# Statistics of two sequences moved from the end of one stage into the next, and a bias split moved behind a plan

## The chip, the cores and the metric

The kernel runs on one core of a Trainium2 chip as one program. Its engines run side by side, each with its own list of instructions, and wait for one another on semaphores: PE (TensorE: matmuls and transposes), DVE (VectorE: elementwise work and reductions), ACT (ScalarE: activation functions), POOL (GpSimd: here products, small arithmetic and DMAs with computed addresses) and SP, which here only issues DMAs. The metric is device time of one execution in microseconds (us); lower is better.

## The reference, cut to what matters

Two transformer layers work on 16 sequences of 512 tokens with 128 features (as 64 tiles of 128 tokens, four to a sequence). Each layer modulates a layer norm, mixes over time, adds, modulates a second layer norm, and applies a mixture of experts:

```python
h = _layernorm(x) * (1 + ca) + sa          # layer 0
x = x + ga * _L0_attn_ref(h, ...)          # a state-space scan, gated, then a layer norm
h = _layernorm(x) * (1 + cb) + sb
x = x + gb * _L0_ffn_ref(h, ...)           # one expert of 8 for each token
h = _layernorm(x) * (1 + ca) + sa          # layer 1: the statistics that the change moves
x = x + ga * _L1_attn_ref(h, ...)          # linear attention with softplus
h = _layernorm(x) * (1 + cb) + sb
x = x + gb * _L1_ffn_ref(h, ...)           # rms norm, then two experts of 8 for each token
```

The layer norm at "layer 1" needs for each token the mean, and one over the root of the variance plus 1e-5. The second matmul of the last mixture adds a bias row per expert, `mlp2_b`.

## The kernel before, in words

The program has four stages, and between them all engines meet at a barrier (`end_phase`: a barrier, clearing of semaphores, a second barrier, L67 to L71). The stages are: the scan's preparation and first norm, the scan itself, layer 0's mixture (L713 to L1146), and layer 1 (from L1149), where attention and the last mixture share one block without a barrier between them. The tokens stay in SBUF in `x_tok`.

**End of layer 0's mixture.** The work is done sequence by sequence in an order written out by hand for each engine. For sequence w, PE multiplies masked features by the experts (`product`), ACT scales the result (`scaled`), PE turns it back (`turn_back`), and DVE adds it to `x_tok` (`added`, L1014). Then come the statistics for the next stage: DVE sums over features (`sum_x2`, L1019), ACT squares and accumulates (`squares_2`, L891, four activations for a sequence), and POOL makes the mean, the root and the shift (`mean_2` L822, `scale_2` L827 to L832) into `rs2` and `shift2`, which live on into the next stage. For the last sequences this chain stands at the very end of the stage.

**Start of layer 1.** SP issues some thirty small DMAs one after another (L1396 to L1422). DVE has a preamble: constants, the split of the key bias into three bf16 pieces (L1826 to L1833), the split of the expert bias `b2` into three bf16 pieces `b2x` (L1834 to L1843), then a wait for three weight DMAs (L1844; the last of them is `gb`, L1410), a few more constants, and the loop over bodies. ACT begins with a load of its function table (L1735). The loop `for n in range(B + ...)` on each engine is a software pipeline: in body n each helper works on sequence n minus its own lag. ACT's `norm0(n)` (L1612) normalizes sequence n with `rs2` and `shift2`, two bodies ahead of PE; DVE's `correction`, `corrected` and `softplus` (L1891, L1898, L1904) make queries and keys, and POOL and PE work on these.

**End of attention.** Each token's row is written to DRAM (`rows_of`) by POOL with DMAs of computed addresses (`send`, L1538, eight to a sequence). DVE makes from the counts the plan of tiles: which tile of the last mixture belongs to which expert and where its rows begin (L2081 to L2122, ending in `packs`). SP waits until all sends have landed (L1452) and then loads the first tiles of rows (`kvb`, L1482); PE, ACT and DVE work on them tile by tile (L2509, L1792, L2191). PE uses `b2x` first with the third tile's step (L2521 to L2526).

Of the kernel before, what the change touches and what calls it, by code (L numbers as in the profile page):

```python
# [13 lines left out]
ACT = mybir.ActivationFunctionType  # L14
AX = mybir.AxisListType

P = 128
D = 128
C = 4
# [5 lines left out]
E = 8  # L25
# [12 lines left out]
def build(nc, a, out):  # L38
    B = a["x"].shape[0]
# [7 lines left out]
    with ctx:  # L47
# [665 lines left out]
        with ExitStack() as sc:  # L713
# [64 lines left out]
            with nc.Block() as block:  # L778
# [39 lines left out]
                def _(pool):  # L818
# [34 lines left out]
                    def mean_2(w):  # L853
                        means(w, "sum2", sum_2, shift2, "mean2")
# [24 lines left out]
                    beta(15); mean_x(14); scale_x(14); mean_2(8); scale_2(8); mean_x(15); scale_x(15); mean_2(9); scale_2(9); mean_2(10)  # L879
                    mean_2(11); mean_2(12); scale_2(10); scale_2(11); scale_2(12); mean_2(13); mean_2(14); scale_2(13); scale_2(14)  # L880
                    mean_2(15); scale_2(15)

                @block.scalar
                def _(act):
# [70 lines left out]
                    squares_2(11); hot_half(15); scaled(12); scaled(13); squares_2(12); scaled(14); squares_2(13); scaled(15)  # L955
                    squares_2(14); squares_2(15)

                @block.vector
                def _(dve):
# [109 lines left out]
                    mask(15, 1); mask(15, 2); mask(15, 3); added(13); mask(15, 4); mask(15, 5); sum_x2(13); mask(15, 6); mask(15, 7)  # L1069
                    added(14); sum_x2(14); added(15); sum_x2(15)  # L1070

# [125 lines left out]
        with ExitStack() as sc:  # L1197
# [70 lines left out]
                     "pay", "pay_ps", "pay_t", "gx", "x4", "lg_ps", "lg_t", "lg_back", "lg", "max", "idx", "idf", "hot", "ed", "ee", "e1", "p1", "taken", "counted", "carried",  # L1268
                     "rank_ps", "rank", "sel", "pos", "posu", "extra", "labels", "totals", "base", "place", "pads", "experts", "plan", "padrow", "beside")
            s = {nm: sem(f"p3_{nm}") for nm in names}  # L1270
            s_rows = [sem(f"p3_rows{u}") for u in range(W)]
            s_scat = [sem(f"p3_scattered{j}") for j in range(PB)]
            counts = sb("counts", [P, E], I32, scope=sc)
            ge, gst = (room[:, q * BT * E3:(q + 1) * BT * E3].rearrange("p (b e) -> p b e", e=E3) for q in range(2))

# [11 lines left out]
            b2f, b2r = (room[0:3, q * E * D:(q + 1) * E * D] for q in range(2))  # L1287
            b2h = sb("b2h", [3, E * D], BF16, scope=sc)
            LAG = 3
            xt = kvb[:, 0:V * S * PAY].rearrange("p (v c d) -> p v c d", v=V, c=S)  # L1290
# [102 lines left out]
            with nc.Block() as block:  # L1393
# [176 lines left out]
                def _(act):  # L1570
# [28 lines left out]
                    def payload(w):  # L1599
                        if exists(w):  # L1600
# [5 lines left out]
                            nc.scalar.activation(pay[w % PB][:, :, D:D + 1], place[:, :].unsqueeze(2), ACT.Copy, bias=float(2 * C * P * w)).then_inc(s["pay"], 1)  # L1606

                    def norm0(w):
                        if exists(w):
                            need(act, "turned", w - 1)  # L1610
                            for c in range(C):
                                last = nc.scalar.activation(nrm0[w % 2][:, c, :], tile(w, c), ACT.Identity, bias=of_tile(shift2, w, c), scale=of_tile(rs2, w, c))  # L1612
                            last.then_inc(s["nrm0"], 1)
# [120 lines left out]

                    nc.scalar.preload_act_table_set("natural_log_exp_and_others")  # L1735
                    for n in range(B + 8):
                        abs_keys(n - 3)
                        exponentials(n - 3)
                        ones_added(n - 3)
                        relu_keys(n - 3)  # L1740
                        values(n - 3)
                        variance_log(n - 6)
                        variance_root(n - 6)
                        logits_kept(n - 8)
                        squares(n - 7)
                        logarithm(n - 3)
                        square_log(n - 7)
                        square_root(n - 7)
                        projected(n - 5)
                        feat(n - 2)  # L1750
                        weigh(n - 8)
                        spread(n - 4)
                        payload(n - 7)
                        turned_pay(n - 7)
                        norm0(n)
                        abs_queries(n - 2)
                        normed(n - 6)
                        relu_queries(n - 2)
# [56 lines left out]
                def _(dve):  # L1815
# [17 lines left out]
                    nc.vector.tensor_copy(bk3[0:3, :, :], bkf[:, :].unsqueeze(1).to_broadcast([3, C, D])).then_inc(s["split"], 1)  # L1833
                    nc.vector.memset(b2x[:, :], 0.0)  # L1834
                    dve.wait_ge(m["bias"], 16)
                    for j in range(2):
                        nc.vector.tensor_copy(b2h[:, :], b2f[:, :]).then_inc(m["split"], 1)
                        dve.wait_ge(m["split"], 3 * j + 1)
                        nc.vector.tensor_scalar(b2r[:, :], b2h[:, :], which[:, j:j + 1], None, ALU.mult).then_inc(m["split"], 1)
                        dve.wait_ge(m["split"], 3 * j + 2)  # L1840
                        nc.vector.tensor_tensor(b2f[:, :], b2f[:, :], b2r[:, :], ALU.subtract).then_inc(m["split"], 1)
                        dve.wait_ge(m["split"], 3 * j + 3)
                    nc.vector.tensor_copy(b2x[0:3, :], b2f[:, :]).then_inc(m["split"], 1)  # L1843
                    dve.wait_ge(s["weights"], 3 * 16)  # L1844
# [88 lines left out]
                    def moments(w):  # L1933
                        if exists(w):
                            need(dve, "x3", w + 1)
                            for c in range(C):
                                last = nc.vector.bn_stats(st[:, c, :], tile(w, c))
                            last.then_inc(s["st"], 1)
                            need(dve, "st", w + 1)
                            need(dve, "lv", w - 1)  # L1940
                            need(dve, "sh", w - 1)
                            for c in range(C):
                                last = nc.vector.bn_aggr(mv[w % 2][:, c, :], st[:, c, :])
                            last.then_inc(s["mv"], 1)

                    def shifted(w):
# [93 lines left out]
                    def numbers():  # L2040
# [11 lines left out]
                        nc.vector.tensor_scalar(beside[:, :, 0], beside[:, :, 0], k("token")[:, 0:1], None, ALU.add).then_inc(s["beside"], 1)  # L2052

                    for n in range(B + 5):
                        weighted(n - 1, 0)
# [21 lines left out]
                        prefixes(n)  # L2077
                        modulated(n - 3)
                        divided(n - 1)
                    need(dve, "totals", 1)  # L2080
# [41 lines left out]
                    nc.vector.tensor_copy(packs[:, :], packf[:, :]).then_inc(s["place"], 1)  # L2122
                    dve.wait_ge(s["plan"], n[0])
                    need(dve, "red", B * C)
                    need(dve, "den", B)
# [473 lines left out]
```

## Time and profile before

| | value |
|---|---|
| three runs, median (lowest to highest) | 977.24 us (975.3 to 979.83) |
| the profiled execution: time, and its span in the trace | 975.13 us, 973.3 us |
| mean granted TensorE clock, as a share of full speed | 0.923 |
| busy share of the span: PE, DVE, ACT, POOL | 85%, 80%, 67%, 58% |
| chain of work that ended last, by engine | PE 46%, POOL 6%, issue 4%, DVE 4%, DMA 2%, ACT 2% |

The time is the whole execution; the span is from the first to the last instruction in the trace, and 1.8 us of this execution lie outside it. A busy share is a mean over stages with different limits. The chain of waits is followed back from the last instruction, at each step to what released it. Stages in the trace: layer 0's mixture from 144.2 to 345.6 us, attention from 345.7 us, and the last mixture's first tile at about 740 us.

### The profile page before, as it was taken

What the parts mean: (1) busy time and instruction counts of PE and PEld (TensorE: products, weight loads), DVE (VectorE), ACT (ScalarE), POOL (GpSimd) and SP (SyncE); (2) the same over time, 40 slices, a digit from 0 to 9 for tenths busy, and PEclk for the clock granted to TensorE, in tenths of its full rate; (3) what the DMA queues carried; (4) which work ended last, traced back from release to release, by engine and by line L of the source; (5) the groups of instructions that cost most, each with busy time, mean ns of one, the idle gap of its engine ahead of it and who ended that gap; (6) DMA issues with size and microseconds to landing.
All of it is one profiled execution on the core that took longest, in us unless ns stands there. A gap on an engine that the chain in (4) does not pass through costs nothing.

```text
span 973.3 us, 23385 instructions
## 1 busy us (share of the span) xinstructions
PE 831.7 (85%) x7407; PEld 642.8 (66%) x7422; DVE 774.2 (80%) x2066; ACT 656.2 (67%) x1731; POOL 561.7 (58%) x571
## 2 busy tenths in 40 slices
PE   6888981799999939999999999999316999999991
PEld 6854651444445428888888888888105988898881
DVE  4987769899998766779999999999762666666896
ACT  3466128899995265667778778774714888888881
POOL 1210009658873324343888888888772666666773
PEclk9989895799999969999999999999557999999996
DMA  5230441242323121000111111111134756655987
GB/s 162 81 93 0 125 143 58 98 148 99 130 99 131 44 52 39 2 1 19 37 35 37 38 39 43 35 35 43 49 101 145 222 183 182 182 178 181 328 262 262
DMA packets 83460, 100.78 MB, mean 104 GB/s; under 512 B 15326, under 2 KB 65305, under 8 KB 81164
## 3 DMA queue, kind: packets, MB, share of 16 engines
q1 hardware_dynamic: 70812, 79.06, 26.6%
q0 software_dynamic: 8640, 17.97, 5.3%
q10 hardware_dynamic: 3888, 2.25, 0.8%
q8 instruction: 62, 1.02, 0.5%
q14 instruction: 58, 0.48, 0.2%
HBM read 75.71 MB, written 23.54 MB: 102 GB/s over the span
## 4 chain that ended last, share of the span: by engine, by line
PE 46%; POOL 6%; issue 4%; DVE 4%; DMA 2%; ACT 2%; SPq 1%; ACTq 0%; POOLq 0%; DVEq 0%
PE ps L2266 11%; PE ps L2509 9%; PE ps L2530 4%; POOL parts L1563 4%; PE ps L2282 3%; POOL rows_of L1538 2%; PE ps L2344 2%; PE ps L2257 2%; PE ps L2228 2%; PE ps L2403 2%; PE ps L2383 2%; PE ps L2277 2%; PE ps L2243 1%; PE ps L2331 1%; PE ps L2492 1%
## 5 line engine op out<-in xcount | busy, mean ns | idle before, releaser
L1529 POOL TENSOR_TENSOR kvb<-qk,v 128x1024 f32<-128x1024 f32 x64 | 126.1, 1975 | 75.9 <-DVE qk L1904 50.4
L1538 POOL DMA_INDIRECT rows_of<-payb,posu x128 | 146.1, 1141 | 39.7 <-issue 27.5
L1115 PE MATMUL ps<-masked,ew 128*128 128x512 f32 x256 | 129.4, 620 | 4.2 <-DVE masked L1043 3.5
L2266 PE MATMUL ps<-con,kvb 128*128 128x128 f32 x1024 | 126.0, 276 | 0.0
L2266 PEld LDWEIGHTS ps<-con,kvb 128*128 128x128 f32 x1024 | 119.4, 192 | 1.0 <-issue 1.0
L2191 DVE TENSOR_SCALAR qk<-ps,b 128x256 f32<-128x256 f32 x142 | 62.0, 478 | 68.5 <-PE ps L2509 65.8
L1563 POOL DMA_INDIRECT parts<-h,dest x72 | 71.2, 989 | 50.3 <-ACT h L1806 34.8
L1043 DVE TENSOR_TENSOR masked<-f_t,wide 128x512 f32<-128x512 f32 x128 | 88.9, 711 | 9.2 <-PE ps L1115 9.0
L1880 DVE TENSOR_TENSOR qc<-ps,qk 128x1024 f32<-128x1024 f32 x64 | 78.0, 1219 | 19.3 <-PE ps L2266 18.7
L1563 POOL DMA_INDIRECT parts<-gx,dest x70 | 72.1, 1030 | 31.7 <-issue 17.7
L2530 PE MATMUL ps<-w,f_t 128*128 x568 | 75.2, 275 | 0.0
L2530 PEld LDWEIGHTS ps<-w,f_t 128*128 128x128 f32 x568 | 69.0, 192 | 8.2
L1115 PEld LDWEIGHTS ps<-masked,ew 128*128 128x128 f32 x256 | 43.2, 193 | 46.8 <-issue 23.3
L1792 ACT ACTIVATE qk<-ps,b 128x256 f32<-128x256 f32 x142 | 59.5, 470 | 17.9 <-PE ps L2509 17.4
L2509 PE MATMUL ps<-qd,ex 128*128 128x256 f32 x288 | 69.7, 386 | 0.0
L2509 PE MATMUL ps<-qd,lg 128*128 128x256 f32 x280 | 66.2, 379 | 0.0
L2509 PEld LDWEIGHTS ps<-qd,ex 128*128 128x128 f32 x288 | 53.0, 194 | 5.9
L891 ACT ACTIVATE junk<-x_tok,stat 128x128 f32<-128x128 f32 x128 | 49.4, 386 | 10.4 <-DVE stat L1019 9.8
L1797 ACT ACTIVATE nrm<-qk,limit 128x512 f32<-128x512 f32 x71 | 51.4, 723 | 7.1 <-ACT qk L1792 0.4
L2157 DVE SCALAR_TENSOR_TENSOR f_t<-qk,nrm 128x512 f32<-128x512 f32 x71 | 49.2, 693 | 7.1 <-DVE qk L2191 0.5
L2509 PEld LDWEIGHTS ps<-qd,lg 128*128 128x128 f32 x280 | 50.5, 190 | 5.4
L2492 PE MATMUL ps<-con,kvb 128*128 128x128 f32 x142 | 27.7, 277 | 26.2 <-DMA kvb<-rows_of 26.2
(347 smaller groups left out, 2127.7 us busy)
## 6 DMA issues: line engine op xcount, KB each, us to landing
wide<-hot_dram SPq DMA_DIRECT2D x16, 1024.0 KB, 4.6
kvb<-rows_of SPq DMA_DIRECT2D x71, 132.0 KB, 2.6
ex<-in_w_dram SPq DMA_DIRECT2D x36, 256.0 KB
lg<-in_w_dram SPq DMA_DIRECT2D x35, 256.0 KB, 2.8
toep<-taps_dram SPq DMA_DIRECT2D x16, 512.0 KB, 5.8
xg<-parts SPq DMA_DIRECT2D x16, 512.0 KB, 5.3
x_tok<-in_x_dram SPq DMA_DIRECT2D x16, 256.0 KB, 3.3
rows<-rows_dram SPq DMA_DIRECT2D x16, 192.0 KB, 3.1
```

The costliest lines, as they stand in the source:

```text
L1043: nc.vector.tensor_tensor(masked[e % 4][:, :], f_t[w % W][:, :], wide[w % W][:, e, :], ALU.mult).then_inc(s["masked"], 1)
L1115: nc.tensor.matmul(ps[:, w % 2, :], ew0[:, e, :], masked[e % 4][:, :], start=False, stop=(e == E - 1)).then_inc(s["product"], 1)
L1529: nc.gpsimd.tensor_tensor(kv[g % KB][:, :, :].rearrange("p e (h d) -> p e h d", h=H), k_in, v_in, ALU.mult).then_inc(s["kv"], 1)
L1538: nc.gpsimd.indirect_dma_start(rows_of, bass.IndirectOffsetOnAxis(ap=posu[w % 2][:, slot, t:t + 1], axis=0), pay[w % PB][:, t, :], None).t ...
L1563: nc.gpsimd.indirect_dma_start(parts, bass.IndirectOffsetOnAxis(ap=dest[:, u, c:c + 1], axis=0), yw[u][:, c, :], None).then_inc(s_out[u], 16)
L1792: last = nc.scalar.activation(glu[v % 2][:, f, :], ps[:, bank, f * SP:(f + 1) * SP], ACT.Relu, bias=b1[:, bass.ds(e * NF + f, 1)], scale=-1.0)
L1797: nc.scalar.activation(gs[v % 2][:, :, :], glu[v % 2][:, :, :], ACT.Gelu_apprx_sigmoid, bias=limit[:, :], scale=-1.0).then_inc(m["gs"], 1)
L1880: nc.vector.tensor_tensor(qc[g % 2][:, :, :], cum(g), q_in, ALU.mult).then_inc(s["qc"], 1)
L2191: last = nc.vector.tensor_scalar(lin[v % 2][:, f, :], ps[:, bank + 1, f * SP:(f + 1) * SP], b1[:, bass.ds(e * NF + 2 + f, 1)], 8.0, ALU.ad ...
L2266: last = nc.tensor.matmul(cum(g)[:, e, :], kv[g % KB][:, e, :], k("upto"), start=True, stop=True)
L2509: last = nc.tensor.matmul(ps[:, bank + f // 2, (f % 2) * SP:(f % 2 + 1) * SP], w1c[v % WC][:, f * P:(f + 1) * P], x_t[v % 2][:, :], start= ...
L2530: last = nc.tensor.matmul(to, act_t[v % 2][:, j, c * P:(c + 1) * P], w2[:, bass.ds(e * (2 * D) + j * D, D)], start=False, stop=(c == S - 1 ...
```

## The change: what it does

1. In layer 0's mixture, `sum_x2`, `squares_2`, `mean_2` and `scale_2` of sequences 14 and 15 are removed (on DVE two reductions, on ACT eight activations, on POOL eight small operations). ACT's table load for layer 1 is issued there, behind `scaled(15)`.
2. In layer 1, DVE computes mean and variance of those eight tiles from `x_tok` directly (`late_moments`), after its preamble and ahead of its first body. ACT makes the root as exp(-0.5 ln(var + eps)) in its body 9 (`late_root`), and DVE the shift in its body 9 (`late_shift`). `norm0` of sequences 14 and 15 waits for it.
3. The split of the expert bias leaves DVE's preamble and stands behind the plan of tiles. Two arrays of the plan move to other columns of the shared room, since the bias now lies in their old place for longer.

```diff
@@ layer 0's mixture
-                    mean_2(11); mean_2(12); scale_2(10); scale_2(11); scale_2(12); mean_2(13); mean_2(14); scale_2(13); scale_2(14)
-                    mean_2(15); scale_2(15)
+                    mean_2(11); mean_2(12); scale_2(10); scale_2(11); scale_2(12); mean_2(13); scale_2(13)
...
-                    squares_2(14); squares_2(15)
+                    nc.scalar.preload_act_table_set("natural_log_exp_and_others")
...
-                    added(14); sum_x2(14); added(15); sum_x2(15)
+                    added(14); added(15)
@@ layer 1
-            ge, gst = (room[:, q * BT * E3:(q + 1) * BT * E3].rearrange("p (b e) -> p b e", e=E3) for q in range(2))
+            ge, gst = (room[:, 2 * E * D + q * BT * E3:2 * E * D + (q + 1) * BT * E3].rearrange("p (b e) -> p b e", e=E3) for q in range(2))
...
+            LATE = 2
+            late_st = sb("late_st", [P, LATE * C, 6], scope=sc)
+            late_mv = sb("late_mv", [P, LATE * C, 2], scope=sc)
@@ ACT
+                    def late_root():
+                        need(act, "init", 3)
+                        need(act, "late_mv", 1)
+                        rs = rs2[:, (B - LATE) * C:B * C]
+                        nc.scalar.activation(rs, late_mv[:, :, 1], ACT.Ln, bias=eps[:, :]).then_inc(s["late_lv"], 1)
+                        need(act, "late_lv", 1)
+                        nc.scalar.activation(rs, rs, ACT.Exp, scale=-0.5).then_inc(s["late_rs"], 1)
...
                     def norm0(w):
                         if exists(w):
                             need(act, "turned", w - 1)
+                            need(act, "late_sh", int(w >= B - LATE))
...
-                    nc.scalar.preload_act_table_set("natural_log_exp_and_others")
                     for n in range(B + 8):
...
                         turned_pay(n - 7)
+                        if n == 9:
+                            late_root()
                         norm0(n)
@@ DVE
-                    nc.vector.memset(b2x[:, :], 0.0)
-                    dve.wait_ge(m["bias"], 16)
-                    for j in range(2):
-                        nc.vector.tensor_copy(b2h[:, :], b2f[:, :]).then_inc(m["split"], 1)
...
-                    nc.vector.tensor_copy(b2x[0:3, :], b2f[:, :]).then_inc(m["split"], 1)
                     dve.wait_ge(s["weights"], 3 * 16)
...
+                    def late_moments():
+                        for j in range(LATE * C):
+                            last = nc.vector.bn_stats(late_st[:, j, :], x_tok[:, (B - LATE) * C + j, :])
+                        last.then_inc(s["late_st"], 1)
+                        need(dve, "late_st", 1)
+                        for j in range(LATE * C):
+                            last = nc.vector.bn_aggr(late_mv[:, j, :], late_st[:, j, :])
+                        last.then_inc(s["late_mv"], 1)
+
+                    def late_shift():
+                        need(dve, "late_rs", 1)
+                        at = slice((B - LATE) * C, B * C)
+                        nc.vector.scalar_tensor_tensor(shift2[:, at], late_mv[:, :, 0], -1.0, rs2[:, at], ALU.mult, ALU.mult).then_inc(s["late_sh"], 1)
...
+                    late_moments()
                     for n in range(B + 5):
...
                         modulated(n - 3)
+                        if n == 9:
+                            late_shift()
                         divided(n - 1)
...
                     dve.wait_ge(s["plan"], n[0])
+                    nc.vector.memset(b2x[:, :], 0.0)
+                    dve.wait_ge(m["bias"], 16)
+                    for j in range(2):
+                        nc.vector.tensor_copy(b2h[:, :], b2f[:, :]).then_inc(m["split"], 1)
+                        dve.wait_ge(m["split"], 3 * j + 1)
+                        nc.vector.tensor_scalar(b2r[:, :], b2h[:, :], which[:, j:j + 1], None, ALU.mult).then_inc(m["split"], 1)
+                        dve.wait_ge(m["split"], 3 * j + 2)
+                        nc.vector.tensor_tensor(b2f[:, :], b2f[:, :], b2r[:, :], ALU.subtract).then_inc(m["split"], 1)
+                        dve.wait_ge(m["split"], 3 * j + 3)
+                    nc.vector.tensor_copy(b2x[0:3, :], b2f[:, :]).then_inc(m["split"], 1)
                     need(dve, "red", B * C)
```

The order of DVE's instructions at the end of layer 0's mixture and in layer 1's preamble, of the kernel before; each row is a line of the program, an operation, what it writes and reads, and its shape (`stat_82` is the sum of `sum_x2`):

```order
L1014 TENSOR_TENSOR x_tok<-x_tok,ps 128x512
L1019 TENSOR_REDUCE stat_82<-x_tok 128x4
L1014 TENSOR_TENSOR x_tok<-x_tok,ps 128x512
L1019 TENSOR_REDUCE stat_82<-x_tok 128x4
L778 UNCONDITIONAL_BRANCH
...
L1833 CAST bk_157<-bkf 3x512
L1834 MEMSET b2x 128x512
...
L1843 CAST b2x<-xg 3x1024
L1845 TENSOR_SCALAR gw<-gw,ns 128x32
...
L1856 TENSOR_SCALAR slot_219<-con 128x8
L1891 SCALAR_TENSOR_TENSOR ex<-lg,ex 128x1024
```

And of the changed kernel, the same place:

```order
L1013 TENSOR_TENSOR x_tok<-x_tok,ps 128x512 x2
L778 UNCONDITIONAL_BRANCH
...
L1845 CAST bk_157<-bkf 3x512
L1847 TENSOR_SCALAR gw<-gw,ns 128x32
...
L1858 TENSOR_SCALAR slot_219<-con 128x8
L1950 BN_STATS late_st<-x_tok 128x6 x8
L1954 BN_AGGR late_mv<-late_st 128x2 x8
L1893 SCALAR_TENSOR_TENSOR ex<-lg,ex 128x1024
```

The two reductions are gone from the stage's end, the bias split is gone from the place ahead of the wait for the weights (which stands in front of the row that writes `gw`), and sixteen statistics stand between the preamble's last constant and the first body's `correction`.

DVE behind the plan of tiles, of the kernel before (`packs` is the plan's result, `qk_183` the first result of the last mixture's first tile on DVE):

```order
L2121 TENSOR_REDUCE packf<-digits 128x9
L2122 CAST packs<-packf 128x9
L2180 TENSOR_LOAD packs
...
L2191 TENSOR_SCALAR qk_183<-ps,b_229 128x256
```

And of the changed kernel:

```order
L2140 TENSOR_REDUCE packf<-digits 128x9
L2141 CAST packs<-packf 128x9
L2143 MEMSET b2x 128x512
L2146 CAST b2h<-xg 3x1024
L2148 TENSOR_SCALAR xg<-b2h,which 3x1024
L2150 TENSOR_TENSOR xg<-xg 3x1024
L2146 CAST b2h<-xg 3x1024
L2148 TENSOR_SCALAR xg<-b2h,which 3x1024
L2150 TENSOR_TENSOR xg<-xg 3x1024
L2152 CAST b2x<-xg 3x1024
L2209 TENSOR_LOAD packs
...
L2220 TENSOR_SCALAR qk_183<-ps,b_231 128x256
```

Eight instructions of the bias split now stand between the plan's result and DVE's first work on tiles.

## Rows read from the trace of the kernel before

**Rows 1.** Timeline, end of layer 0's mixture: start us, us, engine, line, operation, tiles, [idle].

```profile
338.03 0.69 ACT L932 ACTIVATE moe_t<-ps,mod_t 128x512 f32<-128x512 f32 x1 [2.62 <-PE ps L1115]
...
339.52 0.69 DVE L1014 TENSOR_TENSOR x_tok<-x_tok,ps 128x512 f32<-128x512 f32 x1 [3.28 <-PE ps L1103]
...
344.09 0.20 POOL L832 TENSOR_TENSOR shift<-shift,rs 128x4 f32<-128x4 f32 x1
345.68 0.27 SPq L1396 DMA_DIRECT2D bkf<-in_bqkv_dram  x1
...
345.69 1.28 ACT L1735 ACT_TABLE_LOAD   x1 [3.08 <-PEq L70]
```

**Rows 2.** Timeline, the barrier one stage earlier.

```profile
142.19 0.60 ACT L627 ACTIVATE xg<-ps 128x512 f32<-128x512 f32 x1 [1.19 <-PE ps L702]
144.20 0.81 SPq L783 DMA_DIRECT2D rows<-rows_dram  x2
```

**Rows 3.** Chain of waits, start of attention: start us, us, what.

```profile
355.47 2.60 DMA gb<-in_gb_dram
...
358.92 1.24 DVE ex L1891
...
362.81 1.78 PE ps L2403 x6
```

**Rows 4.** Timeline, the bias split in DVE's preamble, and ACT beside it.

```profile
351.21 0.48 DVE L1834 MEMSET b2x<- 128x512 uint32 x1
...
351.63 0.62 DVE L1837 CAST b2h<-xg 3x1024 bf16<-3x1024 f32 x1
...
352.28 0.74 DVE L1839 TENSOR_SCALAR xg<-b2h,which 3x1024 f32<-3x1024 bf16 x1
...
353.06 1.21 DVE L1841 TENSOR_TENSOR xg<-xg 3x1024 f32<-3x1024 f32 x1
...
356.84 1.06 ACT L1664 ACTIVATE lg<-ex 128x1024 f32<-128x1024 f32 x1
357.04 0.68 DVE L1843 CAST b2x<-xg 3x1024 bf16<-3x1024 f32 x1
```

**Rows 5.** Timeline, eight statistics of the first stage in a row on DVE.

```profile
16.57 1.64 DVE L252 BATCH_NORM_STATS2 st<-x_tok 128x6 f32<-128x128 f32 x8
18.24 0.64 DVE L256 BATCH_NORM_AGGREGATE mv<-st 128x2 f32<-128x6 f32 x8
```

**Rows 6.** Timeline, one of ACT's bodies in the middle of attention.

```profile
569.92 1.07 ACT L1651 ACTIVATE v<-ps 128x512 f32<-128x512 f32 x1 [0.40 <-PE ps L2257]
...
570.78 0.27 ACT L1581 ACTIVATE rv<-mv,eps 128x4 f32<-128x4 f32 x1
```

**Rows 7.** Chain of waits, end of attention.

```profile
733.97 2.27 DMA rows_of<-payb,posu
...
738.16 2.08 DMA kvb<-rows_of
```

**Rows 8.** Timeline, POOL's last sends beside DVE's plan.

```profile
715.83 0.96 POOL L1538 DMA_INDIRECT rows_of<-payb,posu  x1 [0.30 <-issue]
...
716.49 0.28 DVE L2097 CAST in_all<-nti 128x24 f32<-128x24 int32 x1
...
718.79 1.96 DVE L2111 TENSOR_TENSOR xg<-number,first 128x1728 f32<-128x1728 f32 x1
719.62 1.96 POOL L1538 DMA_INDIRECT rows_of<-payb,posu  x1 [0.31 <-issue]
...
720.78 1.96 DVE L2113 TENSOR_TENSOR xg<-xg,step 128x1728 f32<-128x1728 f32 x1
...
726.25 0.17 DVE L2122 CAST packs<-packf 128x9 int32<-128x9 f32 x1
726.40 0.96 POOL L1538 DMA_INDIRECT rows_of<-payb,posu  x1 [0.30 <-DMA rows_of<-payb,posu]
...
744.53 0.88 DVE L2191 TENSOR_SCALAR qk<-ps,b 128x256 f32<-128x256 f32 x2 [18.10 <-PE ps L2509]
```

More of the change, by code:

```diff
@@ L1268, in build @@
                      "pay", "pay_ps", "pay_t", "gx", "x4", "lg_ps", "lg_t", "lg_back", "lg", "max", "idx", "idf", "hot", "ed", "ee", "e1", "p1", "taken", "counted", "carried",
-                     "rank_ps", "rank", "sel", "pos", "posu", "extra", "labels", "totals", "base", "place", "pads", "experts", "plan", "padrow", "beside")
+                     "rank_ps", "rank", "sel", "pos", "posu", "extra", "labels", "totals", "base", "place", "pads", "experts", "plan", "padrow", "beside", "late_st", "late_mv", "late_lv", "late_rs", "late_sh")
             s = {nm: sem(f"p3_{nm}") for nm in names}
@@ L1833, in _ @@
                     nc.vector.tensor_copy(bk3[0:3, :, :], bkf[:, :].unsqueeze(1).to_broadcast([3, C, D])).then_inc(s["split"], 1)
-                    nc.vector.memset(b2x[:, :], 0.0)
-                    dve.wait_ge(m["bias"], 16)
-                    for j in range(2):
-                        nc.vector.tensor_copy(b2h[:, :], b2f[:, :]).then_inc(m["split"], 1)
[L1838 to L1842, printed above, removed]
-                    nc.vector.tensor_copy(b2x[0:3, :], b2f[:, :]).then_inc(m["split"], 1)
                     dve.wait_ge(s["weights"], 3 * 16)
```

## The prediction

> **What bounds the kernel now.** The change touches three places, so I read three places and not the busy shares. First the timeline around the barrier behind layer 0's mixture [rows 1, 2]: the reader is to see which engine arrives last, and how long the barrier takes from there. Then the chain of waits at the start of attention, and the timeline beside it [rows 3, 4]: what lets the first body start. Last the chain of waits and the timeline at the end of attention [rows 7, 8]: what lets the last mixture start.
>
> At the barrier POOL is last. Its last shift ends at 344.09 + 0.20 = 344.29, and SP's first DMA of the next stage goes out at 345.68, 1.39 us later [rows 1]. DVE's last addition to the tokens ended at 339.52 + 0.69 = 340.21 [rows 1]. What lies between, 4.08 us, is nothing but the statistics of sequence 15.
>
> At the start of attention the chain runs over SP's row of small DMAs to `gb`, issued at 355.47 and landed at 358.07, then over the rest of DVE's preamble to `correction` at 358.92, and over DVE to PE at 362.81 [rows 3]. The bias split occupies DVE from 351.21 to 357.04 + 0.68 = 357.72 [rows 4], all of it before `gb` has landed. So in the kernel before it costs nothing there.
>
> At the end of attention the chain runs over POOL's sends: the last starts at 733.97 and lands 2.27 later, and from there the first rows are loaded [rows 7]. From `packs` (726.25 + 0.17 = 726.42) to its first work on a tile at 744.53 DVE is idle, 18.10 us [rows 8], while POOL still has the rest of a send and six more to make: seven sends from 726.40 to 733.97, one each 1.26 us.
>
> **Part 1: the statistics leave the end of the stage.** Behind the change the last engine at the barrier is DVE with its addition, which waits for PE and not for anything removed: 340.21. ACT's table load comes behind the scaling that ends at 338.03 + 0.69 = 338.72, and with its 1.28 [rows 1] it is done at 340.00, 0.21 before DVE. POOL has the statistics of sequence 13 left, which hang on squares that ACT makes ahead of 338.03. That POOL was the last to arrive might have made the barrier longer or shorter; one stage earlier ACT was last, at 142.19 + 0.60 = 142.79, and SP's first DMA came at 144.20, 1.41 later [rows 2]. So the next stage starts at 340.21 + 1.40 = 341.61 in place of 345.68: **−4.07 us**. The table load also leaves ACT's start of the stage, 1.28 us. I cost that at nothing: ACT's result for `correction` was ready at 356.84 + 1.06 = 357.90 [rows 4], and DVE came a whole us later, at 358.92. The cover is `gb`; without it at most 1.28 would come on top.
>
> **Part 2: the statistics enter the preamble.** Eight bn_stats and eight bn_aggr of the same shape stand in the first stage: 16.57 to 18.24 + 0.64 = 18.88, so **+2.31 us** [rows 5]. They stand behind the wait for `gb` and ahead of `correction`, that is in the 0.85 us piece of DVE's preamble that the chain goes through, and not in the hole that the bias split leaves (351.2 to 358.07). Queued behind them are `correction`, `corrected` and `softplus`, and behind these POOL's first products and all of PE's first body. So the whole 2.31 moves PE's start at 362.81. It can be 0.1 less where the last aggregate overlaps `correction`, and not below 2.2 as long as DVE works in order; above, I allow 1.0 for a start of PE that falls badly, a little over half of its first piece of 1.78 there [rows 3]. SP's queue is untouched, so `gb` lands as long after the barrier as before. Taken: 2.31.
>
> The root and the shift in body 9: two activations, the larger like L1581, 0.27 us, ahead of `norm0(9)`, and one small operation on DVE. In ACT's body the activation that makes the values waited 0.40 for PE [rows 6]; of some 0.5 at most 0.1 is left, once, with `norm0` two bodies ahead of its user. What could wait for the shift is `norm0(14)`, five bodies later. Zero, or +0.1.
>
> **Part 3: the bias split beside POOL's sends.** DVE itself has 18.10 us of idle time there, and the split takes 357.72 − 351.21 = 6.51 us [rows 4], so it ends at 726.42 + 6.5 = 733; PE uses its result only after the first tile's work at 744.53. But the sends beside it are on the path. What do they suffer? A send that started at 719.62 while DVE's L2111 ran (718.79 to 720.75) took 1.96 instead of 0.96 and ended at 721.58, 0.83 behind L2111's end, with L2113 running from 720.78 [rows 8]. So a send has to read something about 0.13 after its start, an operation with two SBUF inputs holds it up until its own end, and the send gets in between two such operations. The reverse shows too: the cast L2097, started 0.66 into a send, ended at 716.77, with the send (716.79), having taken 0.28 [rows 8]. So the last third of a send and a cast exclude each other. I take both ways: a send waits for a running cast, scaling or subtraction at its read, and for a running cast or scaling at its last third.
>
> Laid on the split's own times [rows 4] moved to 726.45 (memset, cast 0.62, scaling 0.74, subtraction 1.21, cast, scaling, subtraction, cast 0.68): the first send is held 0.41 by the first cast, the second 0.31 by the scaling, the third 0.16 by the second cast, the fourth 0.31 by the second scaling, the fifth 0.17 by the last cast; the sixth and seventh run free. Sum **+1.36 us**. Lower end: if casts hold nothing up, only the two subtractions do, 0.46 and 0.21, 0.67 in all. Nothing makes a send faster, so it isn't below zero. Upper end: if no send gets in until the split is over, the second send reads at about 733.0 and ends at 733.8 in place of 728.6: +5.2.
>
> The Trainium skill (SBUF — State Buffer, "Who interferes with whom") says that a cast, copy or scaling in a two-port mode and GpSimd lock each other out for the whole instruction, and that the one held up comes about 115 ns after the other's end ("A bandwidth-pool intuition that's wrong"). With that estimate, 0.12 on each of five hold-ups would make the 1.36 some 2.0. The trace agrees on the lock for two-input operations; of a long cast beside a send no row here shows anything.
>
> **The sum.** −4.07 + 2.31 + 1.36 = −0.40 us. The profiled execution took 975.13 us (span 973.3 and 1.8 around it), so 974.7 in its place. It was a quick one: the median of the three runs is 977.24, 2.1 above. I forecast for the median **976.8 us**, no change that can be told: 0.5% of 977 is 4.9 us, about what a measurement of this kernel tells from nothing (its own three runs lie within 4.5 us).
>
> **Rivals.** (a) The gain at the barrier stands alone: the sends shrug the split off (+0.67 or less), and the delay at the start of attention is taken up before PE is full. Then −4.07 to −3.4, 973.5 on the median's scale. For it: PE is the largest share of the chain and waits elsewhere too. Against it: the chain has no slack between `gb` and PE [rows 3], and nothing later in the stage waits for a clock of its own that could absorb the shift.
>
> (b) Slower: the split locks POOL out. Its casts, scalings and subtractions follow one another with gaps of 0.03 to 0.04 us [rows 4]. If a waiting send loses each of these gaps, all sends behind the first wait until about 733.0: +5.2, and the sum is −4.07 + 2.31 + 5.2 = +3.4, 980.7. It becomes a loss from the point where the hold-ups exceed 1.76, that is 4.07 − 2.31. Against it: at 720.75 a send did win such a gap, of 0.03 us [rows 8].
>
> The Trainium skill (same page and section) states the block as full and does not say who wins between two instructions that follow at once; by its rule without a hand-over in the gaps the time would be (b)'s.
>
> (c) The change doesn't do what it says at the barrier: another engine arrives at about 344 all the same, say ACT, whose table load is only 0.21 short of being last. Then 0 + 2.31 + 1.36 = +3.7, 980.9. Against it: three engines were seen done, and nothing on SP is left to wait for.
>
> **How the numbers follow.** Forecast 0.65; (a) 0.17; (b) 0.11; (c) 0.04; other 0.03. The forecast's own bounds: −4.07 + 2.2 + 0.67 = −1.2 to −4.07 + 3.3 + 2.1 = +1.3, so 976.0 to 978.5 (2.1: five hold-ups of half an operation, which last 0.84 on average), before the scatter of a median, some 2 us either way. With (a) at the low end and (b) at the high end of it the range is 972.6 to 981.0. Faster by over 0.5% needs a time under 972.4: (a) with a little luck, 0.4 of its 0.17, and 0.05 from the rest, 0.12. Slower needs over 982.1: a third of (b) and (c), and 0.02, 0.07. Within: 0.81.
>
> **What would show it.** Right: the first DMA of attention some 4.1 us earlier (341.6); sixteen statistics between `gb`'s landing and `correction`, which starts about 15.6 us after that DMA instead of 13.2; DVE idle for about 7 us before `gb`; four or five of POOL's last seven sends at 1.1 to 1.4 us instead of 0.96; the first tile's rows at most 1 us from where they were before. Wrong: a barrier that is not earlier, sends of 1.9 us and more in a row, or a last send at its old pace. The forecast as a whole is wrong if the bodies of attention or the tiles of the last mixture take another time each than before, for which I see no cause.

## The result, and the profile after

The changed kernel takes **981.31 us** (median of 20 runs, 976.84 to 984.64) against 977.73 for the kernel before (20 runs, 974.76 to 982.04). The ratio is 1.0031, 95% interval 1.0017 to 1.0045: about **3.0 us slower** (1.7 to 4.4). The forecast was 976.8, range 972.6 to 981.0. So it was wrong in sign, and just outside its range. That the change would stay under 0.5% came true (0.31%), but not by the forecast's sum, and twenty runs of each kernel do tell it from nothing. Ratios are taken over fast runs alone, which leaves out one execution of all those below, e4's of 2173.91 us. The profiled execution of the changed kernel took 979.29 us with a span of 977.5 and a mean clock of 0.924.

Two executions of one kernel differ before attention begins: the last addition at the end of layer 0's mixture lies at 339.52 in the trace of before and at 341.76 in that of after, while the changed kernel run again (e8, below) has it at 339.20. Of what was changed only the reduction for sequence 14 stands ahead of it, and DVE then sat idle for 3.28 us, until PE released the addition [rows 1]. I therefore count from the start of that addition in each trace. The span's 4.2 us are then 2.24 of this scatter, 1.28 up to the load of the first tile's rows, and 0.65 behind it.

The barrier of the changed kernel, in its timeline (start us, us, engine and line, what; the bracket is idle time ahead and what ended it):

```profile
340.26 0.69 ACT L931 ACTIVATE moe_t<-ps,mod_t 128x512 f32<-128x512 f32 x1 [2.61 <-PE ps L1114]
340.97 1.28 ACT L955 ACT_TABLE_LOAD   x1
341.76 0.69 DVE L1013 TENSOR_TENSOR x_tok<-x_tok,ps 128x512 f32<-128x512 f32 x1 [4.00 <-PE ps L1102]
343.81 0.27 SPq L1398 DMA_DIRECT2D bkf<-in_bqkv_dram  x1
```

ACT's table load is done at 342.25, DVE at 342.45, and SP's first DMA comes 1.36 later. From the addition's start to that DMA it is 2.05 us; before it was 345.68 − 339.52 = 6.16 [rows 1]. The barrier gave **−4.11** (forecast −4.07).

The chain of waits at the start of attention answers to [rows 3]:

```profile
353.59 2.61 DMA gb<-in_gb_dram
...
357.05 1.66 DVE late_st L1950 x8
...
358.82 0.54 DVE late_mv L1954 x7
359.36 1.12 DVE ex L1893
...
363.14 1.78 PE ps L2432 x6
```

The statistics stand on the chain, 359.36 − 357.05 = **+2.31**, as forecast. PE starts 21.38 us behind the addition, before 23.29: 1.91 of the 4.11 are left.

In body 9 the shift of the last two sequences, in the timeline of DVE and POOL:

```profile
546.55 0.96 POOL L1540 DMA_INDIRECT rows_of<-payb,posu  x1 [0.30 <-issue]
546.56 0.71 DVE L1974 TENSOR_TENSOR h<-h,rows 128x512 f32<-128x512 f32 x1
547.19 2.35 DVE L1960 SCALAR_TENSOR_TENSOR shift<-late_mv,rs 128x8 f32<-128x8 f32 x1
547.53 1.98 POOL L1531 TENSOR_TENSOR kvb<-qk,v 128x1024 f32<-128x1024 f32 x1
549.47 0.68 DVE L1873 TENSOR_TENSOR g_t<-ps,rb 128x512 f32<-128x512 f32 x1
```

Eight elements per partition took DVE 2.35 us. The operation ends at 549.54 and POOL's product at 549.51: it was held by POOL. Read it by its length, since a held DVE instruction shows as a long one, not as idle time. From here the changed kernel's bodies run late: by the start of `correction`, its lead over before is 1.88 us in body 0 and 2.00 in body 9, then it is 0.12 behind in body 10. From body 11 to body 15 it is 0.31 to 0.46 ahead again. The net cost is **1.5 to 1.7 us**, from an operation that I had at nothing.

The last sends, beside the bias split, answer to [rows 8]:

```profile
727.93 2.00 POOL L1540 DMA_INDIRECT rows_of<-payb,posu  x1 [0.30 <-DMA rows_of<-payb,posu]
...
728.41 0.62 DVE L2146 CAST b2h<-xg 3x1024 bf16<-3x1024 f32 x1
729.06 0.74 DVE L2148 TENSOR_SCALAR xg<-b2h,which 3x1024 f32<-3x1024 bf16 x1
729.84 1.21 DVE L2150 TENSOR_TENSOR xg<-xg 3x1024 f32<-3x1024 f32 x1
730.23 1.66 POOL L1540 DMA_INDIRECT rows_of<-payb,posu  x1 [0.30 <-issue]
...
732.20 1.18 POOL L1540 DMA_INDIRECT rows_of<-payb,posu  x1 [0.30 <-issue]
733.68 0.96 POOL L1540 DMA_INDIRECT rows_of<-payb,posu  x1 [0.30 <-issue]
```

Three sends are held, by 1.04, 0.70 and 0.22, and four run free: **+1.96** where I had 1.36. The first was held through the cast and the scaling behind it, to 729.80 + 0.13, although there are 0.03 us between the two.

### The profile page after: what moved, and what is told of

Same layout as the page of the kernel before. It is cut to its first block, busy times and chain, and to the rows that moved or that the text cites. A ratio compares the mean times of both kernels' runs of the same rounds, so it can differ in the third digit from the quotient of the medians.

```text
span 977.5 us, 23373 instructions
## 1 busy us (share of the span) xinstructions
PE 831.3 (85%) x7407; PEld 642.9 (66%) x7422; DVE 777.1 (79%) x2081; ACT 653.4 (67%) x1717; POOL 560.0 (57%) x563
## 4 chain that ended last, share of the span: by engine, by line
PE 50%; DVE 6%; issue 3%; POOL 2%; DMA 2%; SPq 1%; ACT 1%; POOLq 0%; ACTq 0%; DVEq 0%
PE ps L2538 13%; PE ps L2295 10%; PE ps L2559 6%; PE ps L2311 3%; POOL rows_of L1540 2%; PE ps L2521 2%; PE ps L2373 2%; PE ps L2286 2%; PE ps L2257 1%; PE ps L2432 1%; PE ps L2412 1%; PE ps L2306 1%; PE ps L2272 1%; PE ps L2360 1%; PE ps L2554 1%
## 5 line engine op out<-in xcount | busy, mean ns | idle before, releaser
L890 ACT ACTIVATE junk<-x_tok,stat 128x128 f32<-128x128 f32 x120 | 46.3, 387 | 9.7 <-DVE stat L1018 9.1
```

## The experiments

One table holds what the traces of all runs say. Each number is how much later (+) or earlier (−) the row starts than in the kernel before, both counted from the start of their own last addition (before: first DMA 6.16, `correction(0)` 19.40, eighth-last send 385.62, load of the first tile's rows 397.53).

| run | first DMA | `correction(0)` | eighth-last send | tile's rows | ratio of times [95%] |
|---|---|---|---|---|---|
| changed | −4.11 | −1.88 | −0.71 | +1.28 | 1.0031 [1.0017, 1.0045] |
| e8, changed again | −4.11 | −1.85 | +0.64 | +2.65 | 1.0032 [1.0014, 1.0050] |
| e1, shift moved | −4.11 | −1.89 | −0.85 | +1.14 | 1.0000 [0.9987, 1.0014] |
| e2, split behind sends | −4.11 | −1.74 | −0.62 | −0.61 | 0.9998 [0.9979, 1.0017] |
| e3, moments early | −4.11 | −4.16 | −2.32 | −0.33 | 1.0000 [0.9983, 1.0018] |
| e4, all three | −4.11 | −4.09 | −3.01 | −2.94 | 0.9965 [0.9948, 0.9982] |
| e5, split alone | 0 | +0.05 | +0.90 | +2.95 | 1.0021 [1.0007, 1.0036] |
| e6, three more | −4.11 | −1.91 | +7.50 | +9.50 | 1.0095 [1.0069, 1.0121] |
| e7, one input | −4.11 | −1.89 | −0.44 | +1.56 | 1.0010 [0.9996, 1.0023] |

Behind the load of the tile's rows the traces need 236.0 to 236.9 us to their end, and 237.3 to 237.9 in e1 to e4, which ran in one session; that is not in the order of what was changed. The granted clock of TensorE may account for a part: from that load on it stays at 1.2 GHz for another 7.2 to 8.6 us in e1 to e4, and for 5.5 to 7.0 in the others, but e5, with 8.6 and 236.8, does not fit.

The clock does account for how the lead of the bodies grows behind `correction(0)`. From PE's start in attention to `correction(1)` the kernel before takes 10.45 us, of which 5.72 are granted 1.2 GHz and the rest 2.4; the changed kernel takes 10.23 with 5.26, e3 9.74 with 4.27, and e5 9.35 with 3.50. Less half of the time at 1.2 GHz, each of the ten traces gives 7.59 or 7.60. So what a trace wins there, 0.1 to 1.1 us, comes from when the clock rose, and a single trace says nothing of the change by it.

**e1: the shift where POOL waits for DVE.** It goes behind `shifted(n - 3)`, right after the positions that POOL's next send needs.

```diff
                         shifted(n - 3)
+                        if n == 9:
+                            late_shift()
...
                         modulated(n - 3)
-                        if n == 9:
-                            late_shift()
```

> The changed kernel with one DVE instruction moved: the late shift stands in the same body behind the other shift, where POOL is in a send, and no longer behind the modulation, where POOL runs a product. Theory A (the late shift has two SBUF inputs and is held by POOL's product for 2.2 us, of which the body gives back 0.5): the shift takes 0.15 to 0.25 us in place of 2.35, the jump of 1.7 us between the tenth and eleventh body goes, the time is 1.4 to 1.9 us below the changed kernel, +1.0 to +1.6 against before. Rival (the body loses the time because ACT's two activations of the late root, or any extra instruction, upset it): the jump stays, no change against the changed kernel, +3.0 against before.

Measured: 977.89 us against 977.29, ratio 1.0000 [0.9987, 1.0014]. The timeline of e1:

```profile
538.08 1.01 POOL L1540 DMA_INDIRECT rows_of<-payb,posu  x1 [0.16 <-issue]
538.76 0.30 DVE L2054 CAST posu<-pos 128x8 uint32<-128x8 f32 x1
538.84 0.23 DVE L1966 SCALAR_TENSOR_TENSOR sh<-mv,rv 128x4 f32<-128x4 f32 x1
538.91 0.16 DVE L1960 SCALAR_TENSOR_TENSOR shift<-late_mv,rs 128x8 f32<-128x8 f32 x1
539.83 0.96 POOL L1540 DMA_INDIRECT rows_of<-payb,posu  x1 [0.74 <-DVE posu L2054]
```

The same operation takes 0.16, and the bodies keep a lead of 1.78 to 1.96 to the end; POOL is idle for 0.74 us there, for DVE's own result. So the jump belongs to the place. The table also shows that e1 arrives at the eighth-last send no earlier than the profiled run of the changed kernel: the plan's two large operations held sends by other amounts. First the plan in e1, then in the changed kernel:

```profile
716.72 1.96 DVE L2130 TENSOR_TENSOR xg<-number,first 128x1728 f32<-128x1728 f32 x1
717.00 2.52 POOL L1540 DMA_INDIRECT rows_of<-payb,posu  x1 [0.30 <-issue]
718.72 1.96 DVE L2132 TENSOR_TENSOR xg<-xg,step 128x1728 f32<-128x1728 f32 x1
719.82 1.69 POOL L1540 DMA_INDIRECT rows_of<-payb,posu  x1 [0.30 <-issue]
```

```profile
719.96 0.99 POOL L1540 DMA_INDIRECT rows_of<-payb,posu  x1 [0.30 <-issue]
720.32 1.96 DVE L2130 TENSOR_TENSOR xg<-number,first 128x1728 f32<-128x1728 f32 x1
721.25 1.85 POOL L1540 DMA_INDIRECT rows_of<-payb,posu  x1 [0.30 <-issue]
722.31 1.96 DVE L2132 TENSOR_TENSOR xg<-xg,step 128x1728 f32<-128x1728 f32 x1
723.41 1.69 POOL L1540 DMA_INDIRECT rows_of<-payb,posu  x1 [0.30 <-issue]
```

In e1 a send starts 0.28 us into the first operation and is held for the rest of it; in the other the send starts 0.36 ahead of the operation and runs free, and only the next one is held. The same changed kernel run again (e8) met it like e1, with a send of 2.51. The two sends shown differ by 0.64 us in all; another one, three ahead of them, was held for 0.48 in e1, beside an addition with two SBUF inputs. Together that is worth about 1.1 us, and only the timed runs average over it.

**e2: the split behind all sends.** DVE waits for the sends to land before it starts the split, so nothing of it lies beside one.

```diff
                     dve.wait_ge(s["plan"], n[0])
+                    for j in range(PB):
+                        dve.wait_ge(s_scat[j], 16 * SCATTERS * (B // PB))
```

> The changed kernel with the bias split held back until all of POOL's sends have landed. Theory A (the split costs only by holding sends, 1.96 us in the trace): the last seven sends take 0.96 us each again, the first rows are loaded 1.9 us earlier, +0.9 to +1.4 against before. Rival (the split costs nothing by itself and the time is lost elsewhere; or it now ends too late for DVE's first tile): the sends are quick again but the time is within 0.5 us of the changed kernel, or worse. The split should end some 7 us after the landing, before DVE's first work on a tile.

Measured: 977.95 us against 977.29, ratio 0.9998 [0.9979, 1.0017]. DVE's memset of the split starts at 737.15, the last seven sends all take 0.95 or 0.96, and the rows' load is earlier than before by 0.61, not later by 1.28. The split ends at 743.64, ahead of DVE's first work on a tile at 745.27.

**e3: the statistics in the hole.** `late_moments` goes ahead of the wait for the small weights (`gb` is the last of them).

```diff
+                    late_moments()
                     dve.wait_ge(s["weights"], 3 * 16)
...
-                    late_moments()
                     for n in range(B + 5):
```

> The changed kernel with the sixteen late statistics ahead of the wait for the weights instead of behind it, in the hole of 7 us that the bias split left. Theory A (they cost 2.3 us because they stand in the only piece of the preamble that the chain goes through): correction starts 13.2 us after the first DMA of attention instead of 15.5, the time is 1.9 to 2.3 us below the changed kernel, +0.7 to +1.1 against before. Rival (the delay at the start is taken up later in attention, where PE is full): under 0.5 us below the changed kernel, +2.5 to +3.0 against before.

Measured: 976.09 us against 977.29, ratio 1.0000 [0.9983, 1.0018] (the ratio is not the quotient of the medians: seven of e3's twelve runs lie at 975.2 to 976.3, the others at 978.6 to 982.8). `correction(0)` is 4.16 earlier than before where it was 1.88: the statistics then cost nothing.

**e4: the three together.**

```diff
+                    late_moments()
                     dve.wait_ge(s["weights"], 3 * 16)
...
                         shifted(n - 3)
+                        if n == 9:
+                            late_shift()
...
                     dve.wait_ge(s["plan"], n[0])
+                    for j in range(PB):
+                        dve.wait_ge(s_scat[j], 16 * SCATTERS * (B // PB))
```

> The changed kernel with all three: shift behind the other shift, split after the landing of the sends, statistics ahead of the wait for the weights. Theory A (the four terms add: -4.1 at the barrier stays, +2.3, +1.7 and +1.9 go): -2.8 to -4.0 us against before, 973.7 to 975.0. Rival (the barrier's gain is itself given back in attention, or the 20-run loss has a part upstream of the change): between -1 and +1 against before.

Measured: 974.16 us against 977.29, ratio **0.9965 [0.9948, 0.9982]**, 3.4 us faster than before (1.8 to 5.1). Its timeline:

```profile
351.31 1.63 DVE L1848 BATCH_NORM_STATS2 late_st<-x_tok 128x6 f32<-128x128 f32 x8
352.97 0.64 DVE L1852 BATCH_NORM_AGGREGATE late_mv<-late_st 128x2 f32<-128x6 f32 x8
355.82 0.43 SPq L1412 DMA_DIRECT2D gb<-in_gb_dram  x1
358.47 0.24 DVE L1857 TENSOR_SCALAR gw<-gw,ns 128x32 f32<-128x32 f32 x1 [4.86 <-DMA gb<-in_gb_dram]
...
540.68 0.16 DVE L1961 SCALAR_TENSOR_TENSOR shift<-late_mv,rs 128x8 f32<-128x8 f32 x1
...
726.60 0.96 POOL L1540 DMA_INDIRECT rows_of<-payb,posu  x1 [0.30 <-issue]
727.86 0.96 POOL L1540 DMA_INDIRECT rows_of<-payb,posu  x1 [0.30 <-DMA rows_of<-payb,posu]
```

DVE is through with the statistics before `gb` is even issued and still idles 4.86 us for it. All three causes are then gone, and the gain at the barrier reaches the end but for some 1.1 us, nearly all of it sends that the plan held longer in this execution (one of 2.52).

**e5: only the split moved** (with the columns of the two arrays of the plan), the rest as before.

```diff
-                    nc.vector.memset(b2x[:, :], 0.0)
-                    dve.wait_ge(m["bias"], 16)
-                    for j in range(2):
...
                     dve.wait_ge(s["plan"], n[0])
+                    nc.vector.memset(b2x[:, :], 0.0)
+                    dve.wait_ge(m["bias"], 16)
+                    for j in range(2):
...
```

> The kernel before with the bias split alone moved behind the plan. Theory A (it costs only what it does to the sends, and leaving the preamble gives nothing since gb lands last there): correction starts 13.2 us after the first DMA as before, the first three of the last seven sends take 2.0, 1.7 and 1.2 us, +1.4 to +2.0 against before. Rival (the preamble gains from its leaving, or the sends take it up): -0.5 to +0.5.

Measured: 978.85 us against 976.75, ratio 1.0021 [1.0007, 1.0036], +2.1 us. The sends beside the split in e5:

```profile
726.25 1.99 POOL L1538 DMA_INDIRECT rows_of<-payb,posu  x1 [0.30 <-issue]
728.55 1.66 POOL L1538 DMA_INDIRECT rows_of<-payb,posu  x1 [0.30 <-issue]
730.51 1.18 POOL L1538 DMA_INDIRECT rows_of<-payb,posu  x1 [0.30 <-issue]
732.00 0.96 POOL L1538 DMA_INDIRECT rows_of<-payb,posu  x1 [0.30 <-issue]
```

The same 1.99, 1.66 and 1.18 as in the changed kernel. This part alone makes the kernel slower. In its trace the held sends give 1.98 of the +2.95 at the tile's rows; the +0.90 at the eighth-last send lies ahead of the split. Its bodies run 1.0 to 1.15 us ahead of before from body 1 on. That is the granted clock: (5.72 − 3.50) / 2 = 1.11 by the figures under the table.

**e6: three more such operations.** Bodies 10 to 12 get one each at the old place of the shift. Their result goes to a buffer that nothing reads any more; all else is computed as before.

```diff
                         if n == 9:
                             late_shift()
+                        if n in (10, 11, 12):
+                            nc.vector.scalar_tensor_tensor(late_st[:, :, n - 10], late_mv[:, :, 0], -1.0, rs2[:, (B - LATE) * C:B * C], ALU.mult, ALU.mult)
```

> The changed kernel with three more operations like the late shift (two SBUF inputs of 128x8, into unused space) at the same place of DVE's bodies 10, 11 and 12. Theory A (each is held by POOL's product until its end, 2.2 us, and the body gives 0.5 back): each takes 2.2 to 2.4 us, three further jumps of 1.5 to 1.8 us between bodies, +7 to +9 against before. Rival (the hold is a matter of chance in one body, or is hidden): fewer than two of the three are held, under +5 against before.

Measured: 985.69 us against 976.75, ratio 1.0095 [1.0069, 1.0121]. That is 9.3 us over before, and 6.2 over the changed kernel again (e8, 3.1 in the same session): 2.1 us each on the mean. The view of the tile in e6 (least, median and greatest ns of one, first and last start):

```profile
L2099 DVE SCALAR_TENSOR_TENSOR late_st<-late_mv,rs x3: 2282/2358/2362, 568.4 to 615.8; 128x8 f32<-128x8 f32 x3
```

The further jumps between bodies are 1.68, 1.64 and 5.01 us, and 1.24 of the last come back in the body behind it. The first two are as expected. The last holds two things more: the granted clock was 1.2 GHz for 3.4 us (603.3 to 606.7), and the delay brought another operation with two SBUF inputs, which takes 0.69 elsewhere, up against POOL's product:

```profile
612.57 2.60 DVE L1972 TENSOR_TENSOR h<-h,rows 128x512 f32<-128x512 f32 x1 [0.59 <-ACT h L1731]
612.62 1.98 POOL L1531 TENSOR_TENSOR kvb<-qk,v 128x1024 f32<-128x1024 f32 x1
```

**e7: the same, with one input.** A reduction of the same size in place of each of the three.

```diff
+                        if n in (10, 11, 12):
+                            nc.vector.tensor_reduce(late_st[:, :, n - 10], late_mv[:, :, 0:1], AX.X, ALU.add)
```

> The same with three reductions of one SBUF input of the same size in place of the two-input operations. Theory A (the second SBUF input is what POOL's product holds): each takes 0.15 to 0.25 us, no further jump, +2.5 to +3.7 against before, as the changed kernel. Rival (any further DVE instruction at this place costs): jumps as with two inputs, +7 to +9.

```profile
L2099 DVE TENSOR_REDUCE late_st<-late_mv x3: 155/155/156, 567.3 to 608.0; 128x8 f32<-128x8 f32 x3
```

Measured: 977.89 us against 976.75, ratio 1.0010 [0.9996, 1.0023], +1.0. At the same place an operation with one input takes 0.155 us, and the bodies show the one jump of the shift in body 9 and no other. So it is not an instruction more in DVE's row that costs. A reduction differs from the shift in its kind too, not only in its inputs, but a row of the kernel before settles this: an operation of two inputs, one of them in PSUM, ran beside POOL's product in 46 of its 64 times (in 25 it began while the product ran), and none of the 64 is longer than 1.226 us.

```profile
L1880 DVE TENSOR_TENSOR qc<-ps,qk x64: 1153/1223/1226, 371.3 to 680.0; 128x1024 f32<-128x1024 f32 x64
```

What costs is the second SBUF input beside POOL. The time of e7 came out 1.5 us under the low end of what was expected, which is unexplained; the interval reaches up to +2.2.

**e8: the changed kernel again,** in the session of e5 to e7.

> The changed kernel itself, on the chip and in the session of the next three, for a second look at one execution and a second interval. Theory A (its loss of 3 us is real and sits at the late shift and the sends): +1.7 to +4.5 us against before, again 2.35 us for the shift and 4 us in all on the first three of the last seven sends, less 1.9 or so. Rival (the traced execution was a particular one, and the phase between sends and plan differs from execution to execution): another set of slow sends, another distance from the barrier to the first rows, by more than 0.5 us.

Measured: 979.43 us against 976.75, ratio 1.0032 [1.0014, 1.0050], +3.1. The shift again, in its timeline:

```profile
544.12 0.96 POOL L1540 DMA_INDIRECT rows_of<-payb,posu  x1 [0.30 <-issue]
544.77 2.36 DVE L1960 SCALAR_TENSOR_TENSOR shift<-late_mv,rs 128x8 f32<-128x8 f32 x1
545.11 1.98 POOL L1531 TENSOR_TENSOR kvb<-qk,v 128x1024 f32<-128x1024 f32 x1
```

Its bodies go from a lead of 1.86 to 0.27 behind, and are 0.16 to 0.30 ahead from body 11 to body 15. The jump was not an accident of one execution. The rival is right in part: from the addition to the tile's rows this trace needs 1.37 us more than the changed kernel's first one, most of it sends that the plan held.

## Why the prediction was wrong, step by step

**The barrier, −4.07: right.** −4.11 in every run with this part; DVE was the last engine, the table load 0.20 ahead of it, and the first DMA 1.36 behind. Rival (c) is out. That ACT's table load would be covered at the start of attention was right too.

**The statistics, +2.31: right.** 2.31 on the chain. E3 shows the other half of the argument: in the hole ahead of `gb` they are free, and the piece behind it is where they cost. The prediction named that hole.

**The root and the shift in body 9, "Zero, or +0.1": the step that failed.** The root is small (0.16 in the lead of the bodies). The shift cost 1.5 to 1.7 net. I priced it by its size and asked who waits for its result; I did not ask what POOL does at that moment. It is an operation with two SBUF inputs, which is just what I used in part 3 to explain held sends. The trace of before even has a small one that was caught:

```profile
362.75 1.96 POOL L1529 TENSOR_TENSOR kvb<-qk,v 128x1024 f32<-128x1024 f32 x1 [15.64 <-DVE qk L1904]
362.77 1.97 DVE L1864 SCALAR_TENSOR_TENSOR mod_t<-mod_t,bvo 128x16 f32<-128x16 f32 x1
```

Sixteen elements per partition, 1.97 us, beside POOL's product of 1.96. As an upper bound this row would have moved the sum from −0.40 to +1.4 (1.97 less the 0.16 that it takes alone). The Trainium skill (SBUF — State Buffer, "Who interferes with whom") says that a DVE instruction with two SBUF inputs contends with a GpSimd instruction that reads SBUF; I cited that section for the split and did not lay it on the shift. The trace agrees: 2.35 with two inputs, 0.155 with one (e7).

**The split beside the sends, +1.36: the mechanism right, the size short.** From the eighth-last send to the last it is 10.8 us in place of 8.83 in all seven traces with the split in that place (changed, e1, e3, e5 to e8), that is +1.97, or +1.96 by the three held sends. The mis-sized term is the first send: I had it held by the first cast alone (0.41), and it lost the gap of 0.03 us and waited for the scaling too (1.04). A send did win such a gap behind an operation with two inputs [rows 8]; behind a cast it did not. The second and third sends came at other moments because of that (0.70 and 0.22), and no later one was held (I had five).

**What I said would show the forecast wrong** did show: "the bodies of attention take another time each". One did, body 9. Of the signs for right, two failed: not four or five sends at 1.1 to 1.4 us, but three at 2.00, 1.66 and 1.18, and the first tile's rows 1.28 and 2.65 us (e8) off instead of at most 1. A last send at its old pace was named as a sign for wrong; it came (0.96), but the sum had it running free as well, so it tells nothing.

**Rival (b)** named 980.7, and the time is close to that for the wrong reason. It had 5.2 us of locked sends; they are 1.96. The shift makes up about half of the difference.

**The sum as it should have been:** −4.11 + 2.26 at the start of the bodies (what is left by `correction(0)`, −1.85), +1.6 for root and shift, +1.96 for the sends, is +1.7, and the phase of the sends against the plan adds from −0.4 (the changed kernel's trace) to +0.9 (e8's). That gives +1.3 to +2.6 at the tile's rows, which overlaps the measured 1.7 to 4.4 but stays under its middle of 3.0; 0.4 to 1.7 us are not accounted for. Each of e1, e2 and e3 takes away one term and comes back to the time of before. Each alone so gained some 3.0 us, more than its term in the trace (1.6, 1.96, 2.3) and more than was expected of it. These gains are differences of two ratios from different sessions, with 1.9 to 2.3 us to either side, so the sizes of single terms rest on the traces. Together the three gained 6.5, against 5.9 by the terms.

**Open:** e7's time, the scatter of up to 1.9 us behind the first tile's rows, and what the measured 3.0 has over the sum.

## What to carry to other kernels

Before a small DVE operation is costed at nothing, look at two things: whether it reads two SBUF tiles, and what POOL runs at that moment in the trace; put it where POOL waits for DVE. A cost that is free "beside other work" needs the row of that other work, on every engine that shares something with it. And where one edit moves several pieces, price and try each in its own place: here three pieces took back more than the 4.1 us of the barrier, and nearly nothing at three other places (e4).

## What was not expected of the hardware

A 128x8 operation with two SBUF inputs took 2.35 us on DVE in place of 0.16, in all nine cases that stand at this place of DVE's body (changed, e2, e3, e7, e8, and four in e6; 2.28 to 2.36). In the rows of the changed kernel and of e8 it starts in the last third of a send (546.55 to 547.51; 544.12 to 545.08) and POOL's product follows the send by 0.02 to 0.03 us. So it looks as if the send held it first and the product then went ahead of it. That is read from the rows; it was not tested by itself. In e1 a send ends at 539.09 while the shift runs, and no product follows: 0.16 us.

The indirect send stretches from 0.96 to as much as 2.52 us beside a DVE operation of 1.96 with two inputs, by where in the send the operation starts (0.99, 1.85, 1.96, 2.23 and 2.52 were seen). When held, it is done 0.82 to 0.84 us behind the operation's end (in e1 717.00 + 2.52 = 719.52, against 716.72 + 1.96 = 718.68). An insertion anywhere upstream shifts that meeting and so moves the sends behind it by up to some 1.1 us, with no instruction of its own to show for it.
